# Newton steps of six inverse roots and the last group's low halves moved from VectorE to GpSimd

## The reference

```python
x = x + layernorm(attention(layernorm(x)))      # 16 heads of 64, rotary positions, causal softmax
x = x + layernorm(ffn(layernorm(x)))
# ffn: lin0, SwiGLU, mixture of 8 experts (4 per token, weights normalised) + shared expert,
#      lin1, SwiGLU
def layernorm(x): return (x - mean) / sqrt(var + 1e-5)
```

## Time and profile before

| | |
|---|---|
| Median of 3 runs | 1208.22 us (1207.09 to 1208.79) |
| Profiled execution | 1207.18 us, of which 1205.13 us span of the instructions |
| TensorE busy | 1128.8 us (94%), mean granted clock 0.976 |
| VectorE busy | 994.7 us (83%) |
| ScalarE busy | 939.9 us (78%) |
| GpSimd busy | 938.7 us (78%) |
| Attention | up to about 948 us |
| FFN | from about 953 us |

### The profile page before, as it was taken

The page is one execution under the profiler, slowest core; times in us unless marked ns, Lnnn a source line. Parts: engine busy times, 40 slices in busy tenths (PEclk is TensorE's granted clock), DMA queues, the critical chain, the costliest instruction groups (busy, mean ns, idle before and its releaser), DMA issues. The chain is left out here.

```text
span 1205.1 us, 34913 instructions
## 1 busy us (share of the span) xinstructions
PE 1128.8 (94%) x13543; PEld 790.1 (66%) x13543; DVE 994.7 (83%) x2262; ACT 939.9 (78%) x2180; POOL 938.7 (78%) x980
## 2 busy tenths in 40 slices
PE   4689999999999999999999999999998788999996
PEld 1256677777767777777777777777776555566563
DVE  7799797888879797978879797879789579877987
ACT  3667988889797979789797979788898576656574
POOL 3468899999999999999989999999677445334463
PEclk8699999999999999999999999999999899999999
DMA  6651524262442515252534515152520100000011
GB/s 204 160 141 47 131 65 116 69 141 68 110 116 63 140 38 143 69 125 63 133 85 94 132 46 141 47 132 72 141 68 2 36 1 2 1 2 1 2 36 36
DMA packets 50660, 97.03 MB, mean 81 GB/s; under 512 B 6720, under 2 KB 23360, under 8 KB 48448
## 3 DMA queue, kind: packets, MB, share of 16 engines
q1 hardware_dynamic: 50496, 94.81, 31.5%
HBM read 58.47 MB, written 34.60 MB: 77 GB/s over the span
## 5 line engine op out<-in xcount | busy, mean ns | idle before, releaser
L847 POOL TENSOR_TENSOR Plo<-P,Phi 128x512 f16<-128x512 f32 (+3 forms) x640 | 538.1, 868 | 69.9 <-ACT P L516 66.7
L513 ACT ACTIVATE Phi<-psS 128x512 f16<-128x512 f32 (+3 forms) x768 | 392.5, 511 | 131.2 <-PE psS L368 83.2
L516 ACT ACTIVATE P<-psS 128x512 f32<-128x512 f32 (+3 forms) x640 | 315.1, 493 | 0.0
L392 PE MATMUL psO<-V,Plo 128*128 128x65 f16 x2304 | 288.4, 194 | 0.0
L388 PE MATMUL psO<-V,Phi 128*128 128x65 f16 x2304 | 287.1, 192 | 0.3 <-DVE On L805 0.3
L390 PE MATMUL psO<-V,Phi 128*128 128x64 f16 x2304 | 286.2, 192 | 0.0
L365 PE MATMUL psS<-Q,K 128*128 128x512 f16 (+3 forms) x768 | 251.6, 328 | 12.6 <-DVE Plo L672 9.5
L388 PEld LDWEIGHTS psO<-V,Phi 128*128 128x128 f16 x2304 | 219.7, 98 | 56.7 <-issue 1.0
L368 PE MATMUL psS<-Q,K 65*128 65x512 f16 (+3 forms) x768 | 252.3, 329 | 0.0
L721 DVE TENSOR_REDUCE pmax<-psX 128x1 f32<-128x512 f32 x384 | 242.8, 682 | 1.1 <-PE psX L452 0.6
L390 PEld LDWEIGHTS psO<-V,Phi 128*128 128x128 f16 x2304 | 213.9, 96 | 30.8
(11 more groups left out here) (194 smaller groups left out, 2175.8 us busy)
## 6 DMA issues: line engine op xcount, KB each, us to landing
K<-k_way SPq DMA_DIRECT2D x48, 512.0 KB, 6.9
k_way<-HL SPq DMA_DIRECT2D x64, 256.0 KB, 4.2
q_way<-HL SPq DMA_DIRECT2D x60, 256.0 KB, 3.9
Q<-q_way SPq DMA_DIRECT2D x60, 256.0 KB, 6.8
Q<-q_way SPq DMA_DIRECT2D x15, 512.0 KB, 11.7
out<-y SPq DMA_DIRECT2D x8, 256.0 KB, 2.2
y<-in_x SPq DMA_DIRECT2D x3, 512.0 KB, 10.9
Q<-HL SPq DMA_DIRECT2D x16, 64.0 KB, 4.8
```

The costliest lines, as they stand in the source:

```text
L392: mm = nc.tensor.matmul(O, M.Plo[:, U % NP_, k * P:(k + 1) * P], V[:, HD:2 * HD + 1], start=False, stop=j == t, skip_group_check=True)
L513: nc.scalar.activation(M.Phi[:, U % NP_, 0:w], X, ACT.Exp, scale=SCALE)
L516: nc.scalar.activation(full, X, ACT.Exp, scale=SCALE).then_inc(S.exp_done, 1)
L847: nc.gpsimd.tensor_tensor(M.Plo[:, U % NP_, 0:w], M.P32[:, U % NP_, 0:w], M.Phi[:, U % NP_, 0:w], ALU.subtract).then_inc(S.lo_pool, 1)
```

## The change

- `norm_statistics` is gone; `tile_statistics` may signal `stats_done` at its last instruction, and a new generator `pool_roots` makes the roots on GpSimd: 14 instructions (GpSimd has no fused form here, so that a Newton step is four instructions in place of three), then `roots_done`. Six of the seven calls go there; the output norm of blocks 4 to 6 stays on VectorE.
- In attention GpSimd makes them one instruction a step at `ROOTS_AT`: steps 24 to 37 of group 14 and 18 to 31 of group 15. `AHEAD` is set anew: VectorE's statistics start at step 38 of group 13 and end by step 7 of group 14; shift and residuals begin at step 42 of group 14.
- In the FFN GpSimd makes three instructions a step from n = 5, 13, 23 and 8 steps after `cuts_at[0]`. VectorE's statistics of batch 3's second call start one step later (n = 20), and the shifts stand alone at n = 11, 19, 29 and 14 steps after `cuts_at[0]`.
- `lo_on_pool` takes the whole unit number, and is true for all units of group 15: eight 512-wide low halves go from VectorE to GpSimd, and ScalarE writes the f32 copy of these to SBUF instead of back into psS.

```diff
-AHEAD = ((LAST - 2, 40, 48), (LAST - 1, 0, 8), (LAST - 1, 42, 48), (LAST, 2, 48))
+AHEAD = ((LAST - 2, 38, 48), (LAST - 1, 0, 8), (LAST - 1, 42, 48), (LAST, 2, 17), (LAST, 34, 38))
+ROOTS_AT = ((LAST - 1, 24, 38), (LAST, 18, 32))
...
-    return u % NU not in LO_DVE
+    return U >= SU * LAST or U % NU not in LO_DVE
...
-def tile_statistics(nc, M, chain, src, tiles):
+def tile_statistics(nc, M, chain, src, tiles, done=None):
...
-        if n % 4 == 3:
+        if n % 4 == 3 and (done is None or t != tiles[-1]):
             got = chain.mark(last)
             yield
+    if done is None:
+        chain.seen(got)
+    else:
+        last.then_inc(done, 1)
+        yield
+
+
+def pool_roots(nc, M, S, pool, chain, n, tiles):
+    span = slice(tiles[0], tiles[-1] + 1)
+    std, rstd, half = M.std[:, span], M.rstd[:, span], M.bn[:, span, 0]
+    pool.wait_ge(S.stats_done, n + 1)
+    got = chain.mark(nc.gpsimd.tensor_scalar(std, M.mv[:, span, 1], EPS, None, ALU.add))
+    yield
     chain.seen(got)
+    got = chain.mark(nc.gpsimd.tensor_scalar(rstd.bitcast(I32), std.bitcast(I32), -0.5, ROOT_SEED, ALU.mult, ALU.add))
+    yield
+    for i in range(NEWTON):
+        chain.seen(got)
+        got = chain.mark(nc.gpsimd.tensor_tensor(half, rstd, rstd, ALU.mult))
+        yield
+        chain.seen(got)
+        got = chain.mark(nc.gpsimd.tensor_tensor(half, half, std, ALU.mult))
+        yield
+        chain.seen(got)
+        got = chain.mark(nc.gpsimd.tensor_scalar(half, half, -0.5, 1.5, ALU.mult, ALU.add))
+        yield
+        chain.seen(got)
+        last = nc.gpsimd.tensor_tensor(rstd, rstd, half, ALU.mult)
+        if i == NEWTON - 1:
+            last.then_inc(S.roots_done, 1)
+        else:
+            got = chain.mark(last)
+        yield
...
-                yield from norm_statistics(nc, M, chain, M.y[:, 0:3 * TT], range(3 * TT))
+                yield from tile_statistics(nc, M, chain, M.y[:, 0:3 * TT], range(3 * TT), S.stats_done)
+                dve.wait_ge(S.roots_done, 1)
...
-                yield from norm_statistics(nc, M, chain, M.y[:, 0:2 * TT], range(2 * TT))
+                yield from tile_statistics(nc, M, chain, M.y[:, 0:2 * TT], range(2 * TT), S.stats_done)
+                dve.wait_ge(S.roots_done, 2)
...
+            chain = Chain(pool, S.pool_step)
+            roots = [pool_roots(nc, M, S, pool, chain, n, range(count * TT)) for n, count in enumerate((3, 2))]
             for s, u in steps:
                 U = SU * s + u
-                if s >= 0 and U <= last_unit and lo_on_pool(U % SU):
+                if s >= 0 and U <= last_unit and lo_on_pool(U):
                     low(U)
+                for i, (slot, first, end) in enumerate(ROOTS_AT):
+                    if s == slot and first <= u < end:
+                        next(roots[i], None)
...
-FOURTH_FIRST, ROOT_FIRST, ROOT_PIECES = 1, 10, 2
+FOURTH_FIRST, LATE_FIRST, STAT_PIECES = 1, (10, 20), 2
+POOL_PIECES, ROOTS_FIRST, OUT_ROOTS = 3, (5, 13, 23), 8
+SHIFTS_DUE, OUT_SHIFT = (11, 19, 29), 14
...
-                if n >= ROOT_FIRST:
-                    for _ in range(ROOT_PIECES):
-                        next(after, None)
+                for b in range(2):
+                    if n >= LATE_FIRST[b]:
+                        for _ in range(STAT_PIECES):
+                            next(after[b], None)
+                if n in SHIFTS_DUE:
+                    i = SHIFTS_DUE.index(n)
+                    dve.wait_ge(S.roots_done, i + 1)
+                    if i == 0:
+                        fourth_shift()
+                    else:
+                        shift(range((1 + i) * TT, (2 + i) * TT))
+                if n == cuts_at[0] + OUT_SHIFT:
+                    dve.wait_ge(S.roots_done, 4)
+                    out_shift(0)
...
+                for i in range(4):
+                    if n >= (cuts_at[0] + OUT_ROOTS if i == 3 else ROOTS_FIRST[i]):
+                        for _ in range(POOL_PIECES):
+                            next(roots[i], None)
```

More of the change, by code:

```diff
@@ L210, in seen @@
         self.dve.wait_ge(self.sem, count)
-def norm_statistics(nc, M, chain, src, tiles):
-    yield from tile_statistics(nc, M, chain, src, tiles)
-    yield from norm_roots(nc, M, chain, tiles)
-def tile_statistics(nc, M, chain, src, tiles):
+def tile_statistics(nc, M, chain, src, tiles, done=None):
     for n, t in enumerate(tiles):
@@ L826, in _ @@
                     x_reciprocal()
-                if LOW_FIRST and s >= 0 and U <= last_unit and not lo_on_pool(U % SU):
+                if LOW_FIRST and s >= 0 and U <= last_unit and not lo_on_pool(U):
                     low(U)
@@ L834, in _ @@
                     join_max(s)
-                if not LOW_FIRST and s >= 0 and U <= last_unit and not lo_on_pool(U % SU):
+                if not LOW_FIRST and s >= 0 and U <= last_unit and not lo_on_pool(U):
                     low(U)
@@ L1516, in fourth, with late, fourth_shift @@
             def fourth():
-                tiles = range(3 * TT, NT)
-                yield from norm_statistics(nc, M, chain, M.y[:, 3 * TT:NT], tiles)
+                yield from tile_statistics(nc, M, chain, M.y[:, 3 * TT:NT], range(3 * TT, NT), S.stats_done)
+            def late(b):
+                dve.wait_ge(S.z_sum, TT * (b - 1))
+                if b == 3:
+                    dve.wait_ge(S.y_inverse, 1)
+                yield from tile_statistics(nc, M, chain, M.y[:, b * TT:(b + 1) * TT], range(b * TT, (b + 1) * TT),
+                                           S.stats_done)
+            def fourth_shift():
                 span = slice(3 * TT, NT)
@@ L1522, in fourth, with out_statistics, out_shift @@
                                                in1=M.rstd[:, span], op0=ALU.mult, op1=ALU.mult).then_inc(S.y_inverse, 1)
-                yield
-            def late():
-                for b in range(2, B):
-                    tiles = range(b * TT, (b + 1) * TT)
-                    dve.wait_ge(S.z_sum, TT * (b - 1))
-                    if b == 3:
-                        dve.wait_ge(S.y_inverse, 1)
-                    yield from norm_statistics(nc, M, chain, M.y[:, b * TT:(b + 1) * TT], tiles)
-                    shift(tiles)
-                    yield
-            def out_norm(j):
-                tiles = range(TB * CUTS[j], TB * CUTS[j + 1])
+            def out_statistics(j):
                 for k in range(CUTS[j], CUTS[j + 1]):
                     dve.wait_ge(S.hn_out, k + 1)
-                    yield from tile_statistics(nc, M, chain, R.hn[:, TB * k:TB * k + TB], range(TB * k, TB * k + TB))
-                yield from norm_roots(nc, M, chain, tiles)
-                span = slice(tiles[0], tiles[-1] + 1)
+                    done = S.stats_done if j == 0 and k == CUTS[1] - 1 else None
+                    yield from tile_statistics(nc, M, chain, R.hn[:, TB * k:TB * k + TB], range(TB * k, TB * k + TB), done)
+            def out_shift(j):
+                span = slice(TB * CUTS[j], TB * CUTS[j + 1])
                 got = chain.mark(nc.vector.tensor_tensor(M.mv[:, span, 1], M.mv[:, span, 0], M.rstd[:, span], ALU.mult))
-                yield
                 chain.seen(got)
@@ L1548, in out_norm @@
                                         ALU.subtract).then_inc(S.rstd_ready[0], 1)
+            def out_norm(j):
+                yield from out_statistics(j)
+                yield from norm_roots(nc, M, chain, range(TB * CUTS[j], TB * CUTS[j + 1]))
+                out_shift(j)
             def side(x):
@@ L1648, in _ @@
             routing = [routing_steps(nc, M, S, R, dve, part, part * ROUTE_STEPS) for part in range(2)]
-            final = [out_norm(j) for j in range(len(cuts_at) - 1)]
+            final = [out_statistics(0), out_norm(1)]
             early = max(n for n in at for x in at[n] if x == ("out", 5))
             stats_left = 2 * (TB // 2 + TB // 4)
-            after, first = late(), fourth()
+            after, first = [late(b) for b in range(2, B)], fourth()
             then(nc.vector.tensor_copy(R.w0[:, 0, :], M.wd[:, 0, :]))
@@ L1700, in _ @@
         def _(pool):
+            chain = Chain(pool, S.pool_step)
+            roots = [pool_roots(nc, M, S, pool, chain, i, tiles)
+                     for i, tiles in enumerate((range(3 * TT, NT), range(2 * TT, 3 * TT), range(3 * TT, NT),
+                                                range(TB * CUTS[1])))]
             nc.gpsimd.memset(R.score[:], -1.0).then_inc(S.consts, 1)
```

14 lines of the change are left out of this document (8 added, 6 removed).

## The result

The changed kernel took 1213.58 us (median of 6 runs, 1212.30 to 1215.78) against 1208.47 us (6 runs) for the kernel before: ratio 1.0042 [1.0025, 1.0059], slower by 5.1 us. The forecast was 1200.3 us, range 1196.0 to 1205.5. The profiled execution took 1215.53 us with a span of 1213.5 us (1205.1 before), at a mean granted clock of 0.967 (0.976 before). The two profiled executions lie 8.4 us apart in span, the medians 5.1.

The account below looks back on a forecast made before the run. TensorE bounds up to 897 us, then four chained engines; in the MoE, VectorE's Newton code holds TensorE up. Gains 9.4 less 0.7, 0.3 and 0.5 give 7.9 us: 1208.2 - 7.9 = 1200.3 us, range 1196.0 to 1205.5.

Parts of the forecast that it names:

- the last group: End of attention, from 897 us: low halves end at 942.4 instead of 943.15 us, a gain of 0.7 us.
- My sum for GpSimd's own work: Last attention group: low halves 44.0 us plus roots 2.8 less overlap 3.1, 43.7 us, ending at 941.9.
- Statistics in group 13: Attention, steps 38 and 39: two pieces ahead of the row maxima cost 0.8 us; over 1 us would refute.
- Output norm (3.4): MoE, 1130 to 1147 us: TensorE's gaps in steps with Newton work close, gaining 3.4 us.
- batch 3 (2.8): MoE, 1022.5 to 1037.5 us: TensorE's gaps beside VectorE's Newton work close, gaining 2.8 us.
- Batch 2 (0.8): MoE steps after routing, before 1013.54 us: TensorE's gap closes, gaining 0.8 us.
- Before routing (1.4): Before the first routed sum: Newton instructions leave VectorE, so TensorE's 2.82 us wait becomes 1.4, gaining 1.4 us.
- the clock (1.0): After the first routed sum: the shorter wait probably leaves the clock at 2.4 GHz, gaining 0 to 1.7, taken as 1.0 us.
- GpSimd's small instructions: The 84 moved Newton instructions on GpSimd: 0.2 us each, upper end 0.43 us.
- chain of three a step: MoE steps: three dependent GpSimd instructions put it 1 to 2 us behind, mostly covered; cost 0.3 us.
- the rival of 1212.2 us: GpSimd's Newton chain delays low halves in the MoE and last group, giving 1212.2 us; chance 0.07.
- The lone shifts (0.7): FFN steps 11, 19, 29 and output norm: shifts standing alone each meet the SBUF wait, costing 0.7 us together.

Follow-up runs that it names:

- GpSimd made late: The FFN's part alone with all last-group low halves on GpSimd, plus 14 small GpSimd instructions at steps 18 to 31: 1198.96 us, 0.9937.
- late tiles: The change with VectorE's eight normalised tiles moved behind the last output scaling of attention: 1211.25 us, 1.0028.
- the pause: The change with GpSimd waiting for VectorE's tile pair before unit 35's low half: 1206.65 us, 0.9983; with four such waits 1208.60 us, 1.0000.
- low halves alone: The FFN's part alone plus all low halves of the last group on GpSimd, attention's roots on VectorE, old windows: 1198.09 us, 0.9912.
- the FFN's part alone: The changed kernel with the attention of before, keeping only the change's FFN: 1201.21 us, 0.9939.
- roots with the old window: The change with low halves shared as before and the statistics in the old window, roots on GpSimd: 1199.86 us, 0.9925.
- steps 42 to 45 and the old statistics window: The change with the normalised tiles at steps 42 to 45 of the last group and statistics in the old window: 1208.27 us, 1.0000.
- GpSimd's roots and shared low halves: The change with VectorE keeping its 8 low halves of the last group, roots on GpSimd: 1204.19 us, 0.9955.

## Why the prediction was wrong

**The step that failed** is the last group: "VectorE's traffic on the same memory has stretched low halves by a tenth here and there, so +0.5: the end at 942.4". I asked only what VectorE's accesses do to GpSimd's low halves. The other direction decided: what an unbroken run of GpSimd does to VectorE, and what is queued behind VectorE's instruction. The end was 959.08, and what VectorE waits had no term at all. My sum for GpSimd's own work was not the fault: with the same low halves and 14 small instructions (GpSimd made late) attention ended at 943.74. The largest piece is the passed-over tile: 7.75 us at the end with the late tiles, and some 7 in time by the pause; that this tile and the scaling behind it make the loss is shown by the pauses, which leave all of GpSimd's and VectorE's work in place and only let the tile in.

What else there is I read from the waits and windows of the kernel after: 3.3 us of later start of group 14 (its first scores start at 849.25 us for 845.95 before; 0.6 of it was there at 834 us already, ahead of all that the change moved); 3.0 us of a scaling behind the residual tiles (1.1 with the low halves alone); 2.7 us for GpSimd; less 5.3 us of the old wait that did go. With the 7.8 us of TensorE's wait these make 11.5 of the 15.9 us. The remaining 4.4 I put down to the clock, which no run tests. It fell behind each of the two waits for the scaling, and TensorE, which has hardly a gap in these stretches, lost there by the rows below (an estimate) 5.5 x 0.48 + 4.5 x 0.50 = 4.9 us:

```profile
910.50:916.00 5.50, 5.48 (x63) 4.69 (x64) 4.26 (x32) 2.20 (x7) 2.90 (x4) 0.52 0.00 0
954.60:959.10 4.50, 4.41 (x60) 4.25 (x61) 0.46 (x2) 1.59 (x5) 1.09 (x2) 0.50 0.01 4
```

**Statistics in group 13:** priced 0.8 us, measured 3.6 and 3.1 in time. I had named this as a way to be wrong ("if the statistics moved into group 13 delay the row maxima by more than 1 us"): the wait itself was 1.1 us, and the clock fell after it, which I had not priced.

**FFN:** forecast 9.4 - 0.7 - 0.3 = 8.4; measured 7.5 between the two profiles, 7.2 by the FFN's part alone. That the total came close is in part luck, as two errors offset each other. From the first routed sum's product to the end the FFN took 200.8 us before and 192.4 after, 8.5 us less, with 7.0 forecast there (3.4 + 2.8 + 0.8 + 1.0 less 0.7 and 0.3); from the end of attention to that product it took 61.2 before and 62.1 after, 0.9 us more, with 1.4 less forecast. Term by term:
- Output norm (3.4) and batch 3 (2.8): right. Expert steps of 1.96 us (1142.00 to 1143.96 below); waits for the gating from 1135 to 1165 us are 0.3 us, and from 1024 to 1055 us none.
- Batch 2 (0.8): too small. TensorE's waits for the gating before 1013.54, 1015.94 and 1018.34 us (0.60, 0.26 and 0.26 us) are all gone, with 0.16 us for each as in the forecast 1.6 us.
- Before routing (1.4) and the clock (1.0): wrong. The wait stayed 2.81 us and the clock fell behind it as before, 0.57 for 0.53. (The forecast read 0.53 as "half of it at the 1.2 GHz level"; a mean of 0.53 is nearly all of the stretch at that level. Its loss of 1.7 us is rightly worked out.) VectorE did begin the last part of the routing 0.45 us earlier relative to TensorE's product, but the multiplication that makes the routing weights took 0.84 us in place of 0.29, and the one on the scores 1.25 in place of 1.03. In this stretch the waits for SBUF were not a property of the Newton code: taken off it, they fell on the next instructions with two SBUF inputs. What was saved was only the instructions' own time.
- The clock in the first FFN steps: no term had it. It fell there after the change and not before, where 953 to 973 us had 1.00; the kernel with the FFN's part alone has the same two values (0.83 and 0.66). Why is open. In the kernel after:

```profile
969.00:979.00 10.00, 7.39 (x25) 3.56 (x22) 5.86 (x11) 7.26 (x11) 7.09 (x12) 0.83 0.38 106
979.00:989.00 10.00, 9.42 (x37) 5.88 (x38) 6.35 (x25) 6.37 (x15) 4.00 (x5) 0.66 0.01 2
```

- GpSimd's small instructions: right, 0.20 to 0.28 us (0.2 priced). Its chain of three a step delayed nothing: no product of the FFN waited for GpSimd, so the rival of 1212.2 us, which came close to the time, had the wrong mechanism. The lone shifts (0.7) cost no wait that TensorE shows.

TensorE, single steps of the FFN after:

```profile
1021.14 1.08 PE L1384 MATMUL psY<-ws,hid 128*128 128x128 f16 x12 [2.81 <-DVE moe L1659]
...
1142.00 0.81 PE L1353 MATMUL psG<-h1s,ws 128*128 128x512 f16 x3
...
1143.29 0.83 PE L1384 MATMUL psY<-ws,hid 128*128 128x128 f16 x12
1143.96 0.81 PE L1353 MATMUL psG<-h1s,ws 128*128 128x512 f16 x3
```

VectorE, the multiplication that makes the routing weights, after:

```profile
1019.00 0.84 DVE L1221 TENSOR_TENSOR comb<-left,small 128x128 f32<-128x128 f32 x1
```

GpSimd in one step of the output norm:

```profile
1144.38 1.16 POOL L1786 TENSOR_TENSOR hid<-hid 128x512 f16<-128x512 f32 x1
1145.49 0.24 POOL L251 TENSOR_TENSOR bn_xy<-bn_xy,std_xy 128x16 f32<-128x16 f32 x1
1145.81 0.23 POOL L254 TENSOR_SCALAR bn_xy<-bn_xy 128x16 f32<-128x16 f32 x1
1146.13 0.23 POOL L257 TENSOR_TENSOR rstd_xy<-rstd_xy,bn_xy 128x16 f32<-128x16 f32 x1
```

## What to carry to other kernels

- When work moves to an engine that shares an access with another, price both directions: what the other's accesses do to it, and what the run of instructions that it now makes without a pause does to the other, together with all that is queued behind the instruction that waits.
- Two parts of a change that are harmless alone (low halves alone 0.9912, roots with the old window 0.9925) lost 0.7% or more against either of them when they stood together (1.0000 and 1.0042); test the parts and the whole. A short wait put into the filling engine (0.42 us) won back more than ten times its price here.
- Removing an instruction that is seen waiting for a shared access may remove only its work: before the first routed sum the wait fell on the next instruction with two SBUF inputs, while in the output norm it went, and a step took 1.96 us for 2.76. Look which instruction comes next.

## What the runs showed of the hardware that I had not expected

- One VectorE instruction of 0.33 us (128x128 f32, SBUF to SBUF) took 12.47 us beside 14 consecutive GpSimd instructions, and 12.47, 12.475, 12.47 and 12.48 us in four other kernels; 11.36 beside 13, and 9.4 with steps 42 to 45 and the old statistics window. It is always the first normalised tile; the seven behind it did not wait so.
- The Trainium skill (SBUF — State Buffer, SBUF: two separate sides) says that of a GpSimd instruction and a VectorE instruction that runs in a two-port mode or has two SBUF inputs, whichever starts first has the shared ports for the whole instruction, and the other is blocked. The traces agree for one instruction (waits up to 1.2 us behind low halves of 1.16); a lock for one instruction at a time does not explain 14.
- What singles that tile out stays open. In the cases whose ready inputs I read it was passed over when GpSimd had the inputs of two or more further low halves ready and VectorE had not had such an access for 6.5 us or more, and got in when none or one was ready. With two ready and an access 1.5 us before it got in as well, so the lead alone is refuted; the wait for the roots, the stepped output and the width of the next low half have no part in it. That a recent turn protects is one reading of a single case, and was not tested by itself. Nor was the other reading, that GpSimd must have made the roots: in every kernel with a passed-over tile it had. That alone is not enough, as with GpSimd's roots and shared low halves the longest tile took 1.19 us.
